# A longer ring of gathered edge tiles and fewer TensorE signals in three message passes of a graph network

## The reference

```python
# layer 1
w = alpha[rel, 0]
support = x @ weight
out = segment_sum(w[:, None] * support[col], row)
out = out + segment_sum(w[:, None] * support[row], col)
return out + bias
# layer 2, twice, with leaky_relu(0.1) between
msg = x[src] @ W_msg + b_msg
agg = segment_sum(msg, dst)
return agg + x @ W_self + b_self
```

## Time and profile before

| | us |
|---|---|
| median of 3 runs | 10775.97 |
| lowest, highest | 10763.34, 10826.26 |
| the profiled execution, its own time | 10739.69 |
| its span | 10737.9 |
| PE, DVE, POOL busy | 6092.5, 4834.7, 5352.2 |

### The profile page before, as it was taken

How to read it: one execution, slowest core, us unless ns; L and a number is a source line. 1 busy time by engine, 2 the same in 40 slices (tenths; PEclk the granted TensorE clock), 3 DMA queues, 4 the chain that set the end, 5 groups by cost and what they waited for, 6 DMA issues and landing times. The chain is left out here.

```text
span 10737.9 us, 135754 instructions
## 1 busy us (share of the span) xinstructions
PE 6092.5 (57%) x24674; PEld 4803.9 (45%) x24675; DVE 4834.7 (45%) x13534; ACT 2017.8 (19%) x5480; POOL 5352.2 (50%) x5364
## 2 busy tenths in 40 slices
PE   4788886775656666645554555555555642222376
PEld 2777774554444444433332343334343432222254
DVE  6344446776544444445554333343233411112777
ACT  2111111783322222200000000010000300000276
POOL 3555551000078888866664666636666146664000
PEclk9688877997877777766666676677676755555699
DMA  4555555662077777754443333222323156665265
GB/s 148 160 165 162 161 162 190 199 201 80 18 111 105 105 105 104 105 125 135 133 135 100 88 88 87 87 78 86 86 86 87 40 154 195 194 197 158 72 201 181
DMA packets 835352, 1362.46 MB, mean 127 GB/s; under 512 B 112278, under 2 KB 488660, under 8 KB 834980
## 3 DMA queue, kind: packets, MB, share of 16 engines
q0 software_dynamic: 315328, 634.04, 26.7%
q1 hardware_dynamic: 385684, 562.46, 16.0%
q10 hardware_dynamic: 133968, 161.50, 4.7%
HBM read 943.05 MB, written 414.50 MB: 126 GB/s over the span
## 5 line engine op out<-in xcount | busy, mean ns | idle before, releaser
L1014 POOL DMA_INDIRECT rows_in<-table,gather_rows x2352 | 2250.9, 957 | 1276.4 <-issue 618.2
L1111 PE MATMUL ps_p<-rows_in,hot 128*128 x5280 | 1783.1, 494 | 1708.2 <-issue 758.9
L1111 PEld LDWEIGHTS ps_p<-rows_in,hot 128*128 128x128 f32 x5280 | 1236.8, 247 | 2211.0 <-issue 2014.6
L1740 POOL DMA_INDIRECT scatter_sums<-regionC,idx x880 | 1384.3, 1573 | 306.5 <-issue 248.1
L959 DVE TENSOR_TENSOR regionC<-regionC,ps_p 128x257 f32 (+2 forms) x1320 | 558.2, 423 | 1537.7 <-DVEq L956 846.1
L1014 POOL DMA_INDIRECT regionB<-table,gather_rows x784 | 783.4, 999 | 637.6 <-POOLq L1011 431.5
L1480 PE MATMUL ps_p<-regionA 128*128 128x265 f32 (+1 forms) x3520 | 849.0, 394 | 335.6 <-PEq L1475 215.0
L1014 POOL DMA_INDIRECT regionC<-table,gather_rows x784 | 759.7, 969 | 476.8 <-POOLq L1011 242.9
L1945 PE MATMUL psS<-dst_scores,regionA 128*128 x1760 | 393.3, 362 | 882.7 <-PEq L1943 648.8
L1480 PEld LDWEIGHTS ps_p<-regionA 128*128 128x128 f32 x3520 | 654.0, 191 | 530.6 <-DVE regionC L959 194.0
L1945 PEld LDWEIGHTS psS<-dst_scores,regionA 128*128 128x128 f32 x1760 | 383.6, 330 | 892.4 <-issue 892.4
(11 more groups left out here) (304 smaller groups left out, 7652.8 us busy)
## 6 DMA issues: line engine op xcount, KB each, us to landing
regionA<-edge_rows SPq DMA_DIRECT2D x880, 256.0 KB, 3.2
edge_rows<-regionB SPq DMA_DIRECT2D x196, 512.0 KB
edge_rows<-regionC SPq DMA_DIRECT2D x392, 256.0 KB
regionC<-srcrow_d SPq DMA_DIRECT2D x220, 256.0 KB
scatter_sums<-zero_rows ACTq DMA_DIRECT2D x8, 6400.0 KB, 41.5
regionA<-scatter_sums ACTq DMA_DIRECT2D x49, 1024.0 KB
rows_in<-table,gather_rows POOLq DMA_INDIRECT x2352
regionB<-rrow_d ACTq DMA_DIRECT2D x110, 256.0 KB
```

What stands on the lines that cost most here:

```text
L1014: g.indirect_dma_start(out=rows_of(b * per + j), out_offset=None, in_=table, in_offset=bass.IndirectOffsetOnAxis(ap=idx[:, column:column + ...
L1111: x = te.matmul(ps[(u.c * VG + j) % NB][:, 0:width], hot[:, b, 2 * j + k, :], at_tile(G, slot[j] * 2 + k), start=k == 0, stop=k == 1)
L1740: g.indirect_dma_start(out=scat, out_offset=bass.IndirectOffsetOnAxis(ap=idx[:, b, j:j + 1], axis=0), in_=sums[:, b, j, :], in_offset=None ...
```

## The change

The ring of the plain passes has 12 groups (48 tiles) and lies in a region that is free: C in 'l1', B in 'l2a' and 'l2b'. SyncE frees a group ten groups behind. Six PSUM banks hold twelve products, two in each bank. TensorE waits once for a unit (adds of the unit three before, landing of its last group) and signals once, with the count `s_units`; SyncE waits on the same count, by a table `units_by`, before it frees a group. One-hots have four sets, and VectorE adds unit u-3 in turn u. In layer 2, ring and x cannot both be in B, so x goes to HBM beside `ln_stats` and comes back at the start of the second convolution's dense loop. The degree column moves from 'l2a' to layer 0's attention sum, 266 columns in place of 265, and regionB grows to NT * 266 elements in each partition.

```diff
-RG, RG0 = (6, 8)
+RG, RG0 = (12, 8)
...
-        def landed_groups(sp, s_rows, used, unused, ring, keep=None, kept=None):
-            behind = ring // 2
+        def landed_groups(sp, s_rows, used, unused, ring, behind, by, top, keep=None, kept=None):
...
-                done = sp.value_load(visits_by[0:1, bass.ds(u.val, 1)], min_val=1, max_val=NV)
+                done = sp.value_load(by[0:1, bass.ds(u.val, 1)], min_val=1, max_val=top)
...
-            NB = 4
+            NB, HB, LATE = (12, 4, 3)
...
-                G = sb('rows_in', [P, RG * EG, width], F32, ctx)
+                G = part(room, 0, [RG * EG, D])
-                hot = sb('hot', [P, 2, GS, P], F32, ctx)
+                hot = sb('hot', [P, HB, GS, P], F32, ctx)
-                ps = [bank(f'ps_p{i}', ctx) for i in range(NB)]
+                banks = [bank(f'ps_p{i}', ctx) for i in range(NB // 2)]
+                ps = [banks[i // 2][:, i % 2 * D:(i % 2 + 1) * D] for i in range(NB)]
...
-                        landed_groups(sp, s_rows, s_add, NB, RG)
+                        landed_groups(sp, s_rows, s_units, 0, RG, RG - 2, units_by, NU)
...
                             te.wait_ge(hot_full[b], 1)
                             te.sem_inc(hot_full[b], -1)
+                            te.wait_ge(s_add.sem, (u.val + 1) * VG + s_add.base)
+                            te.wait_ge(s_landed.sem, (last_group & 255) + s_landed.base)
                             for j in range(VG):
-                                te.wait_ge(s_landed.sem, (group[j] & 255) + s_landed.base)
-                                te.wait_ge(s_add.sem, u.val * VG + (j + 1) + s_add.base)
                                 for k in (0, 1):
-                                    x = te.matmul(ps[(u.c * VG + j) % NB][:, 0:width], ...)
-                                x.then_inc(step_full, 1)
+                                    x = te.matmul(ps[(u.c * VG + j) % NB], ...)
+                            x.then_inc(s_units.sem, 1)
...
-                            for t_ in turns(te, NU, 2, 0, ...):
-                                own_trans(t_.at(0))
-                                multiply(t_.at(0))
-                                own_mm(t_.at(0))
+                            for t_ in turns(te, NU, 4, 1, ...):
+                                if t_.has(1):
+                                    multiply(t_.at(1))
+                                    own_mm(t_.at(1))
+                                if t_.has(0):
+                                    own_trans(t_.at(0))
...
                         def adds(u):
-                            add_visits(v, u, regs, acc, ps, width, NB)
+                            nt = of_visits(v, node_of, u.val * VG, regs, NT - 1)
+                            v.wait_ge(s_units.sem, u.val + 1 + s_units.base)
+                            for j in range(VG):
+                                v.wait_ge(s_add.sem, u.val * VG + (j + NB) + s_add.base)
+                                x = at_tile(acc, nt[j])
+                                v.tensor_tensor(x, x, ps[(u.c * VG + j) % NB], ALU.add).then_inc(s_add.sem, 1)
...
-                            for t_ in turns(v, NU, 2, 1, ...):
+                            for t_ in turns(v, NU, 4, LATE, ...):
+                                if t_.has(2):
+                                    own_out(t_.at(2))
                                 if t_.has(0):
                                     hots(t_.at(0))
-                                if t_.has(1):
-                                    adds(t_.at(1))
-                                if t_.has(1):
-                                    own_out(t_.at(1))
+                                if t_.has(LATE):
+                                    adds(t_.at(LATE))
...
+        def put_away(sp):
+            for g in range(GT):
+                sp.dma_start(x_d[g * GT * P:(g + 1) * GT * P, :]..., B256[:, g * GT:(g + 1) * GT, :]).then_inc(s_st.sem, 16)
+                s_st.base += 16
+
+        def bring_back(sp):
+            for g in range(GT):
+                sp.dma_start(B256[:, g * GT:(g + 1) * GT, :], x_d[g * GT * P:(g + 1) * GT * P, :]...).then_inc(s_x[g], 16)
+        ln_stats(B256, put_away)
...
         def post_conv1(v, u, ps, rows):
             y = at_tile(A256, u.val)
-            dg = ACC1[:, bass.ds(u.val, 1), D:D + 1].rearrange('p a c -> p (a c)')
-            v.tensor_copy(deg[:, bass.ds(u.val, 1)], dg)
+            dg = deg[:, bass.ds(u.val, 1)]
...
         def post_conv2(v, u, ps, rows):
-            x = at_tile(B256, u.val)
-            v.tensor_tensor(x, x, at_tile(A256, u.val), ALU.add)
+            x, y = at_tile(B256, u.val), at_tile(A256, u.val)
+            v.scalar_tensor_tensor(out=y, in0=rows[:, 0, :], scalar=deg[...], in1=y, op0=ALU.mult, op1=ALU.add)
-            v.scalar_tensor_tensor(out=x, in0=rows[:, 0, :], scalar=deg[...], in1=x, op0=ALU.mult, op1=ALU.add)
+            v.tensor_tensor(y, y, ps[:, 0:D], ALU.add)
-            return v.tensor_tensor(x, x, ps[:, 0:D], ALU.add)
-        dense_loop(1, D, conv_weights(2), sums_pre(C256), post_conv2, nrows=1)
+            if u.val % GT == 0:
+                v.wait_ge(s_x[u.val // GT], 16)
+            return v.tensor_tensor(x, x, y, ALU.add)
+        dense_loop(1, D, conv_weights(2), sums_pre(C256), post_conv2, nrows=1, first_in=bring_back)
```

110 lines of the change are left out of this document (60 added, 50 removed).

## The result

The kernel after took 10655.27 us (median of 4 runs, 10629.75 to 10664.35), the kernel before beside it 10777.65 us (4 runs): ratio 0.9862, 95% interval 0.9833 to 0.9892 (the ratio and its interval are those on record; the two medians divided give 0.9886). By the medians it is 122 us faster, where the forecast had 305 us less. The range of the forecast, 10220 to 10680 us, holds it, near the end that was worked out for no trickle at all. The profiled execution took 10629.75 us, against 10739.69 us before.

The account below looks back on a forecast made before the run. Bound: a cycle of gather run, held signals, 24-tile ring used up, pause, costing 594 us. Terms -364 + 35 + 3 + 25 - 7.5 + 3 + 1 = -304.5 took the 10776 us median to 10470 us; range 10220 to 10680.

Parts of the forecast that it names:

- no trickle at all: Plain passes: nothing worked off late in gather runs; 27.5 pauses, 146 us a pass, giving the range's upper end, 10680 us.
- the trickle in the runs: Plain passes: some units worked off during unbroken gathers, leaving pauses of 50, 90 and 90 us, 230 for 594: -364 us.
- my two readings: Plain passes: either the single signal is slow (pauses 0 and 67 us) or the work behind it (94 and 114).
- The second reading: Plain passes: the work behind a signal is slow, trickle 0.048 and 0.031 units per us, pauses of 94 and 114 us.
- Signals: Plain passes: by the Trainium skill's 26.3 ns per increment, 330 fewer signals are worth 9 us a pass, 27 in three.
- Tails: End of each plain pass: 4 us and four units of 4.25 us after the last gather, 21 us; +35 for three passes.
- x: Layer 2: x to HBM beside ln_stats, +3 us; back ahead of the second convolution's weights on SP's queue, +25 us.
- Degree: First conv loop: the degree copy at L2264, 49 of 154 ns, goes away: -7.5 us.
- Column and small terms: One more attention column and seven small copies, +3 us; preamble integers, unrolled loops, reordered operations and half-bank products, +1 us.
- A: Plain passes: whole-unit signals keep up and pauses vanish, 594 us gained in place of 364, total 10240; chance 0.22.
- B: Plain passes: unit signals held until GpSimd stops, pauses of 7.14 us, passes of 1250 us, total 10950; chance 0.08.
- C: Plain passes: own_out ahead of one-hots in layer 2, folding in l1; passes 1130 to 1190 us, total 10640 to 10800; chance 0.17.

Follow-up runs that it names:

- e2: Kernel after with one TensorE signal per visit again (440 a pass, not 110), ring of 48 tiles kept: 10593.63 us, ratio 0.9881 to the kernel before.
- e15: Kernel after with four open products in l1, 512-byte rows in l2a, a memset ahead of each eight gathers in l2b: 10737.89 us, ratio 0.9947.
- e1: Kernel after with its ring back at 24 tiles, all else unchanged: 10561.36 us, ratio 0.9850 to the kernel before.
- e18: Kernel after with a 24-tile ring, x's first 26 tiles left in place, conv2's weights issued first: 10565.10 us, ratio 0.9848.
- e12: Kernel after with conv2's weights issued ahead of the seven transfers of x, on a chip without pauses: 9512.88 us, ratio 1.0025.
- e5: Kernel after, unchanged, on a chip without pauses: 9523.76 us, ratio 1.0030 to the kernel before.
- e3: Kernel after with only the first of each visit's two matmuls in the plain passes: 10559.56 us, ratio 0.9848 to the kernel before.
- e9: Kernel before, unchanged, run again on a chip without pauses: 9490.05 us, ratio 0.9998.

## Why the prediction missed

**What bounds the passes** was right on that chip: pauses of a gather that would take 992 us undisturbed. Three other chips showed that very figure. The cycle (run, little gets through, ring used up, pause) was right in outline, and so was its key: what counts is what one pause lets through. Twelve open products work, four give nothing.

**The step that failed is the trickle in the runs: the term of 50, 90 and 90 us of pauses, -364 in the sum.** I took values between my two readings (0 and 67 us, 94 and 114 us), since one signal in place of four might be held no longer than one and so let whole units through during a run. Measured against 992 us a pass, as the forecast counted, the pauses are 139, 153 and 152 us, 444 in place of 230: of the term of 364 only 150 came, and 214 are missing. Against the 146 us of a pass without any trickle, the forecast had it worth 96, 56 and 56 us; by the measured lengths it was worth 7, -7 and -6, which is nothing. e2 shows that the number of signals is free, so thinning them could not help. The bound that I had written down for no trickle at all was 146 us a pass and 1138 in length: the three passes came to 1131, 1145 and 1144. That it fits so well is in part luck, for its cycle of 27 pauses of 5.3 us after runs of 36 us did not come: there are twice as many pauses, half as long, with runs of 15 to 18 us. I take it that a group of four tiles that comes free ends a pause long before three units are worked off; no run tests that.

The reading of the rows behind it, "TensorE's word reaches VectorE late", was right as far as it went: in the kernel before, finished products do lie unused, 79 times in l2a. Wrong was to put this down to the signal as such. TensorE's own steps can be slow instead, 2 to 3 us apart as in the timeline above, and the pass is then as long.

The second reading ("the work behind a signal is slow", pauses of 94 and 114 us) was nearer. The row that I had called the nearest, the score loop of layer 3, with 0.018 units per us, said so, and I set it aside for its DMA load. e15 shows that the load does not matter in a plain pass: 45 GB/s or 90 GB/s, its length is about the same. To give that row its weight was the thing to do.

**Signals.** The Trainium skill (TensorE: Matmul & The Clock Gate, The cost: per-tile semaphore tail) prices an increment at 26.3 ns, by an estimate 9 us for the 330 of a pass and some 27 us for the three passes. e2 puts 330 increments a pass back, and its passes are 1121.3, 1133.6 and 1131.8 us against 1127.7, 1138.6 and 1134.6 in e1 on the same chip, which differs in the ring as well: the 9 us a pass do not show. The reason is argued only: a pass that waits for other things need not grow by TensorE's own time.

**Tails**, +35: measured +12. l1 ends 17.1 us after its last gather's end in place of 12.1; in the others SyncE's next issue comes 3 and 4 us later than before. The units were in hand as forecast, five of them in l1, and the first add came 3.6 us after the last gather's end (5779.1). But from the second on they went at 2.43 us each, not 4.25, since the one-hots are made by then:

```profile
5782.68 2.11 DVE L1189 TENSOR_TENSOR regionB<-regionB,ps_p 128x256 f32 x4 [12.91 <-remote]
...
5791.62 2.11 DVE L1189 TENSOR_TENSOR regionB<-regionB,ps_p 128x256 f32 x4 [0.33 <-DVE regionB L1189]
5794.05 2.11 DVE L1189 TENSOR_TENSOR regionB<-regionB,ps_p 128x256 f32 x4 [0.33 <-DVE regionB L1189]
```

**x**, +3 out and +25 back: out cost nothing, back +18.6 in ScalarE's start, of which +13.4 is left in the length of conv2. The place was right: weights behind seven issues of 12.36 us, against the earlier trace rows:

```profile
8267.61 12.36 SPq L2252 DMA_DIRECT2D regionB<-x_kept  x7
8280.01 2.55 SPq L189 DMA_DIRECT2D weights<-in_L_gnn_W_msg  x1
...
8290.02 0.72 ACT L2286 ACTIVATE src_tile<-regionC 128x256 f32<-128x256 f32 x2 [136.54 <-ACTq L522]
```

e18 takes most of this back.

**Degree**, -7.5: conv1 is 5.1 us shorter. **Column and small terms**, +4: the first gather of l1 starts 5 us later (4647.1 against 4642.1). Layer 3's gathers took 16 us longer than in the profile of before, but this stage is the same in both kernels, and took 1244 to 1264 us in the profiles of the chips with pauses. Sum: -150 + 12 + 13 - 5 + 5 + 16 = -109, against 109.9 between the two spans.

**The rivals.** A (no pauses) didn't come about; nor did B: the longest wait at the ring in l2b was 7.8 us, but the pauses averaged 2.8 us, and no pass became slower. C had the size, passes of 1130 to 1190, and in part the reason. In l2b VectorE does wait for the own product ahead of one-hots, and TensorE for VectorE's adds:

```profile
DVE regionA L1195 <- DVEq L1194: 475.5, 36, 29.3
...
PE ps_p L1128 <- DVE regionC L1189: 278.6, 37, 24.7
...
POOL regionB L1028 <- POOLq L1025: 161.5, 103, 7.8
```

(waits of l2b: us, times, longest.) l1, which has no own products, has nearly the same pauses (131 against 149), which speaks against C. But l1 has 145 slow steps of TensorE and l2b only 27, and no late adds, so in l2b the delay lies elsewhere, and the chain of the own product is where the waits are. A version with own_out behind the adds was not tried, so for layer 2 rival C's reason stays open.

**What stays open** is why chips differ. On those with pauses the queues of TensorE and perhaps VectorE get on slowly beside unbroken gathers, and on the three without they don't, with the same program. No run says what makes it so, nor whether it belongs to the chip at all. Open too is what slow steps and late adds have in common, which must be what sets the length, since one takes the other's place and the pass stays the same.

## What to carry to other kernels

When instructions come one by one with nothing that they wait for, or finished products lie unused, while another engine runs without a break, look first at how much work is ready to go in each gap: here signals, ring and bytes gave nothing, and open products gave the gain. One timeline is not enough to say which engine is slow; count over a pass, and over the variants. Time such a change on more than one chip before keeping it: the one here is worth 1.1 to 1.4% on some and costs 0.3% on others. And transfers put ahead of a stage's weights on the same queue hold the stage up; issuing the weights first helps little while the start signal stands behind the transfers (e12). Leave in place what the stage needs first (e18).

## What the runs showed of the hardware

- Two kinds of chip, each chip seen once. The kernel before took 9488.39 to 9494.46 us on three chips and, in four comparisons on at least three chips, 10718.83 to 10801.16 us (medians). The runs of one group agree within 1%, and the two kinds never mixed in a group. The gather is 946 and 949 ns at the median on the two; 1195 of the 1247 us between the two profiles lie where gathers run.
- On the slower kind TensorE at times makes a matmul record in 2.1 to 2.9 us in an unbroken run of gathers; the register work ahead of a matmul, 0.06 us at most in l1 of e5, takes up to 1.41 us there. e5, on the other kind, makes 16 records in 5.40 us beside the same gathers:

```profile
4823.15 5.00 PEld L1128 LDWEIGHTS ps_p<-regionC,hot 128*128 128x128 f32 x16 [4.38 <-issue]
4823.16 5.40 PE L1128 MATMUL ps_p<-regionC,hot 128*128 x16 [3.99 <-SPq L992]
4824.04 0.98 POOL L1028 DMA_INDIRECT regionC<-table,gather_rows  x1 [0.30 <-POOLq L1025]
```

- On the slower kind VectorE's adds can begin up to 13.4 us after TensorE's last matmul (e3, l1), with VectorE idle for over 1 us of it. In e5 and e9, on the other kind, none of the adds counted began more than 2 us after it.
- About 93 us of memsets added to GpSimd's 1144 us pass cost 4 us on the slower kind, and 104 us on the faster.
- Granted clock did not decide: in l1, TensorE had 0.67 with twelve open products and 0.75 with four (e15), and the latter pass is 57 us longer; in layer 3's stage it is 0.50 on both kinds of chip, 1245 against 1032 us.
